# Two attention layers taken through five stages instead of four, with separate PSUM banks for maxima and scores and the rows normalised on GpSimd

## The reference

```
x: (32, 256, 256)   context: (32, 120, 256)   16 heads of width 16

layer 0:  h = layernorm(x)
          q = rope(h @ Wq); k = rope(context @ Wk); v = context @ Wv
          x = x + tanh(g[0]) * (softmax(q k^T / 4) v @ Wo + bo)

layer 1:  h = layernorm(layernorm(x)) * g + b;  c = layernorm(context) * g' + b'
          q = h @ Wq.T; k = c @ Wk.T; v = c @ Wv.T
          gate = sigmoid(h @ Wg.T + bg)
          x = x + tanh(g[1]) * ((softmax(q k^T / 4) v) * gate) @ Wo.T
```

## Time and profile before

| | |
|---|---|
| median of 3 runs | 3047.76 us (3045.49 to 3053.43) |
| the profiled execution | 3043.93 us, of which 3042.1 us are the span of the trace |
| busy over the whole span | PE 2019.0 us, DVE 1762.6, ACT 1315.4, POOL 1003.7 |
| attention, layer 0 | from the start to about 787 us |
| experts | to about 1515 us |
| attention, layer 1 | to about 2346 us |
| granted PE clock, mean over the execution | 0.81 |

### The profile page before, as it was taken

The page is one execution under the profiler, slowest core; times in us unless marked ns, Lnnn a source line. Parts: engine busy times, 40 slices in busy tenths (PEclk is TensorE's granted clock), DMA queues, the critical chain, the costliest instruction groups (busy, mean ns, idle before and its releaser), DMA issues. The chain is left out here.

```text
span 3042.1 us, 49795 instructions
## 1 busy us (share of the span) xinstructions
PE 2019.0 (66%) x14617; PEld 1560.7 (51%) x14617; DVE 1762.6 (58%) x3650; ACT 1315.4 (43%) x2345; POOL 1003.7 (33%) x1096
## 2 busy tenths in 40 slices
PE   5777677777543199999938788887886334444443
PEld 4555555555433199999825566665664222222222
DVE  5666666666454233333225555555553898988887
ACT  3444333344211044444324444444443566666665
POOL 0000100001266522222243333333330465565554
PEclk8988888888655599999968999999998566666666
DMA  2111111110443322222243333333331000000000
GB/s 68 40 36 43 36 39 36 37 43 26 141 154 125 123 76 87 87 87 87 77 82 65 69 80 71 69 68 67 76 70 56 17 27 28 28 21 28 28 25 17
DMA packets 177265, 185.56 MB, mean 61 GB/s; under 512 B 23745, under 2 KB 170946, under 8 KB 176130
## 3 DMA queue, kind: packets, MB, share of 16 engines
q1 hardware_dynamic: 152578, 149.49, 16.5%
q0 software_dynamic: 24576, 34.62, 5.6%
HBM read 109.82 MB, written 74.24 MB: 61 GB/s over the span
## 5 line engine op out<-in xcount | busy, mean ns | idle before, releaser
L527 DVE TENSOR_REDUCE a_mneg<-a_ps_s 128x8 f32<-128x960 f32 x256 | 285.8, 1151 | 63.0 <-PE a_ps_s L681 62.5
L681 PE MATMUL a_ps_s<-a_k,a_q 96*128 96x240 bf16 x1024 | 189.5, 334 | 153.9 <-DVE a_of L538 149.6
L377 ACT ACTIVATE a_probs<-a_ps_s 120x1024 f32<-120x1024 f32 x256 | 250.2, 1018 | 84.3 <-PE a_ps_s L695 84.3
L1295 DVE TENSOR_TENSOR e_h<-e_s,e_ps_ab 128x256 f32<-128x256 f32 (+1 forms) x213 | 89.4, 420 | 293.4 <-ACT e_s L1121 293.4
L1086 POOL TENSOR_TENSOR e_h_lo<-e_h 128x256 bf16<-128x256 f32 (+1 forms) x213 | 130.2, 611 | 326.0 <-DVE e_h L1295 326.0
L1314 PE MATMUL e_ps_ab<-e_xt_hi,e_w_hi 128*128 128x256 bf16 (+1 forms) x852 | 232.8, 273 | 0.1
L1314 PE MATMUL e_ps_ab<-e_xt_hi,e_w_lo 128*128 128x256 bf16 (+1 forms) x852 | 232.7, 273 | 0.0
L1314 PE MATMUL e_ps_ab<-e_xt_lo,e_w_hi 128*128 128x256 bf16 (+1 forms) x852 | 232.7, 273 | 0.0
L313 POOL TENSOR_TENSOR a_ve<-a_mv,a_eps 128x2 f32<-128x2 f32 x32 | 6.2, 195 | 664.7 <-DVE a_mv L506 664.7
L681 PEld LDWEIGHTS a_ps_s<-a_k,a_q 96*128 96x128 bf16 x1024 | 118.0, 121 | 195.2 <-DVE a_of L538 104.8
L341 POOL DMA_INDIRECT a_xa<-back_rows,a_where x128 | 202.2, 1580 | 45.8 <-issue 44.3
(11 more groups left out here) (237 smaller groups left out, 5430.8 us busy)
## 6 DMA issues: line engine op xcount, KB each, us to landing
e_xe<-sent_rows SPq DMA_DIRECT2D x71, 272.0 KB, 2.8
back_rows<-e_yo SPq DMA_DIRECT2D x71, 256.0 KB, 2.1
x_rows<-a_x SPq DMA_DIRECT2D x64, 256.0 KB, 3.2
a_xa<-in_x SPq DMA_DIRECT2D x32, 256.0 KB, 2.7
a_xr<-in_x SPq DMA_DIRECT2D x32, 256.0 KB, 2.9
e_xa<-x_rows SPq DMA_DIRECT2D x8, 1024.0 KB, 10.6
a_xa<-x_rows SPq DMA_DIRECT2D x32, 256.0 KB, 2.8
x_rows<-a_xa SPq DMA_DIRECT2D x32, 256.0 KB, 2.6
```

The source lines that it names most:

```text
L377: nc.scalar.activation(probs[0:S, 4 * g:4 * g + 4, :].rearrange("p h n -> p (h n)"), ps_s[0:S, g % 2, :, :].rearrange("p a n -> p (a n)"), ...
L527: nc.vector.tensor_reduce(mneg[:, g // 2, 8 * (g % 2):8 * (g % 2) + 8].rearrange("p (a h) -> p a h", a=2), ps_s[:, g % 2, :, 0:4 * S].rear ...
L681: last = nc.tensor.matmul(ps_s[:, g % 2, j // 2, (j % 2) * 2 * S:(j % 2 + 1) * 2 * S], q2[0:96, back.par, c, t * P:(t + 1) * P], k2[0:96, ...
```

## The change

There is one stage more, `mid`. It takes the maxima products, the maxima, their transposition and the gate projection out of `back` and `front`; `back` keeps the scores, the exponentials and the weighing. The order of the work in each engine's `step` is written anew.

- PSUM: `ps_m` (two banks, maxima) and `ps_e` (two banks, scores and weighed values) take the place of `ps_s`. The transposes of `raw` go to `ps_t` and `ps_x`.
- Maxima are taken for 4 heads at a time (eight instructions a batch in place of four), exponentials for two heads (eight of 512 columns for four of 1024), and the division is made in two halves.
- GpSimd computes `xn` and `cn`; the two gathers of layer 1 stand on both sides of it.
- The copy of query columns 4 to 7 (`q2b`) goes from DVE to ACT, and `xt` has two buffers.
- Signals `dv`, `da` and `de` belong to the stage `mid`; `tv` now covers the division too.

```diff
-        ps_s = psum("ps_s", [P, 2, 2, 512])
+        ps_m = psum("ps_m", [P, 2, 512])
+        ps_e = psum("ps_e", [P, 2, 512])
...
-                pipeline(eng, lambda *batches: step(None, *batches), 4, 6)
+                pipeline(eng, lambda *batches: step(None, *batches), 5, 6)
             else:
-                pipeline(eng, step, 5, 6)
+                pipeline(eng, step, 6, 8)
...
+                ng.wait(gp, pre, "rstd")
+                fe.wait(gp, pre.back(1), "xT")
+                nc.gpsimd.tensor_tensor(ready[:, :], half[:, 0:1], half[:, 0:1], ALU.mult).then_inc(ng.sem, 1)
+                for t in range(NT):
+                    last = nc.gpsimd.tensor_scalar(xn[:, t, :], xa[:, p, t, :], mv[:, t, 0:1], rstd[:, t:t + 1],
+                                                   ALU.subtract, ALU.mult)
+                if not first:
+                    last = nc.gpsimd.tensor_scalar(cn[0:S, :], ca[0:S, p, :], mv[0:S, NT, 0:1], rstd[0:S, NT:NT + 1],
+                                                   ALU.subtract, ALU.mult)
+                last.then_inc(ng.sem, 1)
...
+                def maxima():
+                    de.wait(act, mid, "mT")
+                    bv.wait(act, mid.back(1), "m_all")
+                    nc.scalar.activation(mt[:, :], ps_t[0:2 * H, 0:N // 2].bitcast(BF16), ACT.Copy).then_inc(da.sem, 1)
...
+                def turn_back(i):
+                    if i == 0:
+                        ba.wait(pe, tail, "raw")
+                        da.wait(pe, back, "mT")
                     else:
+                        fa.wait(pe, mid, "q2a")
+                        tv.wait(pe, tail.back(1), "sum")
+                    to = (ps_t, ps_x)[i]
+                    for g in range(H // GH):
+                        last = nc.tensor.transpose(to[:, g * P:(g + 1) * P], raw[:, g, i * P:(i + 1) * P], ident[:, :])
+                    last.then_inc(te.sem, 1)
...
+                def gate_rows():
+                    if t:
+                        tv.wait(pe, tail, "sum")
+                    elif f:
+                        fa.wait(pe, front.back(1), "q2a")
+                    for i in range(NT):
+                        last = product(ps_x[:, i * D:(i + 1) * D], terms(xt[:, mid.par, :, :], slice(i * P, (i + 1) * P), wq, D) + bias_terms)
+                    last.then_inc(de.sem, 1)
```

More of the change, by code:

```diff
@@ L186, in attention @@
         s_half = sem(tag + "half")
[L188 to L202, removed]
+        nv = Signal(sem(tag + "nv"), "stats mean")
@@ new lines, in attention @@
+        dv = Signal(sem(tag + "dv"), tops + " m_hi m_lo")
+        da = Signal(sem(tag + "da"), "mT" if first else "gate mT")
+        de = Signal(sem(tag + "de"), " ".join(f"ms{i}" for i in range(8)) + (" mT" if first else " g mT"))
+        bv = Signal(sem(tag + "bv"), "m_all")
+        ba = Signal(sem(tag + "ba"), " ".join(f"exp{i}" for i in range(NP)) + " raw")
+        be = Signal(sem(tag + "be"), " ".join(f"sc{i}" for i in range(NP)) + " pv")
+        tv = Signal(sem(tag + "tv"), "recip0 o0 recip1 o1 sum" if first else "recip0 o0 recip1 o1 gated sum")
@@ L310, in norms @@
             def norms(pre):
-                nv.wait(gp, pre, "mean1" if first else "mean2")
+                p = pre.par
+                nv.wait(gp, pre, "mean")
                 if first:
@@ L369, in _, with step, rows @@
             act.wait_ge(s_low, N_CONST_POOL)
[L371 to L386, removed]
+            def step(soon, pre, front, mid, back, tail):
+                f, m, b, t = front is not None, mid is not None, back is not None, tail is not None
+                def rows():
+                    p = front.par
+                    if first:
+                        fe.wait(act, front, "xT")
+                        fe.wait(act, front.back(2), "q")
+                        nc.scalar.activation(xt[:, p, :, :].rearrange("p k n -> p (k n)"), ps_q[:, :], ACT.Copy).then_inc(fa.sem, 1)
+                        return
                     fe.wait(act, front, "cT")
@@ L418, in keys @@
                                          ACT.Copy).then_inc(fa.sem, 1)
-                def maxima():
-                    be.wait(act, back, "mT")
-                    bv.wait(act, back.back(1), "m_all")
-                    nc.scalar.activation(mt[:, :], ps_t[0:2 * H, 0:N // 2].bitcast(BF16), ACT.Copy).then_inc(ba.sem, 1)
-                if f and not first:
-                    keys()
-                if b:
-                    maxima()
-                if f and first:
-                    keys()
                 def queries():
@@ L463, in step, with gating @@
                                          ACT.Copy, scale=pairmask[0:96, 0:1]).then_inc(fa.sem, 1)
+                    fe.wait(act, front, "qTb")
+                    nc.scalar.activation(q2[0:96, p, 4:8, :].rearrange("p c n -> p (c n)"), ps_kv[0:96, :].bitcast(BF16), ACT.Copy).then_inc(fa.sem, 1)
                     fe.wait(act, front, "qTa")
                     nc.scalar.activation(q2[0:96, p, 0:4, :].rearrange("p c n -> p (c n)"), ps_x[0:96, :].bitcast(BF16), ACT.Copy).then_inc(fa.sem, 1)
+                def gating():
+                    de.wait(act, mid, "g")
+                    tv.wait(act, mid.back(2), "gated")
+                    nc.scalar.activation(gate[:, mid.par, :, :].rearrange("p t d -> p (t d)"), ps_x[:, :], ACT.Tanh, scale=0.5).then_inc(da.sem, 1)
+                def maxima():
+                    de.wait(act, mid, "mT")
+                    bv.wait(act, mid.back(1), "m_all")
+                    nc.scalar.activation(mt[:, :], ps_t[0:2 * H, 0:N // 2].bitcast(BF16), ACT.Copy).then_inc(da.sem, 1)
+                if f:
+                    rows()
+                if b:
+                    for i in range(4):
+                        exp(i)
+                if t:
+                    result()
+                if b:
+                    exp(4)
+                if f:
+                    keys()
+                if b:
+                    exp(5)
+                    exp(6)
+                if f:
+                    queries()
+                if b:
+                    exp(7)
+                if m and not first:
+                    gating()
+                if f:
+                    values()
+                if b:
+                    turned_raw()
+                if f:
+                    columns()
+                if m:
+                    maxima()
             staged(nc.scalar, step)
```

532 lines of the change are left out of this document (274 added, 258 removed).

## The result

The changed kernel takes 3131.41 us (median of 4 runs, 3126.0 to 3133.52), the kernel before, beside it on the same chip, 3049.76 (4 runs). The ratio is 1.0266, with a 95% interval of 1.0245 to 1.0286. The forecast was 3132. That nearness is luck: the change to layer 0 gained some 44 us more than forecast, the one to layer 1 cost some 44 more, and the two errors cancel.

What follows compares the result with a forecast made beforehand. No engine but a ring of waits bounds the kernel. Steps of 21.0 and 28.8 us against 23.80 and 23.94, 29 each, plus 12 a layer, give -69 and +153; with 3043.9 and 3.8 that makes 3132, range 2980 to 3200.

Steps and rivals of the forecast that it cites:

- The clock ahead of the gate: Layer 1, gate projection after PE waits for the sum: low clock adds 1.2 us a step, between 1.0 and 1.8.
- Item (4) of the ring of layer 1: Layer 1, ACT after the gate projection: gate 0.6, then the values, for which the weighing waits; 1.05 us.
- item (3) of layer 0: Layer 0, ACT ahead of the weighing: query copy, last exponential and values, 1.5 us.
- both rings: Chains of last-ending waits through one step, at full clock: 19.1 us in layer 0, 25.75 us in layer 1.
- The clock at the step's end: Both layers, PE pausing during ACT's final copies: the clock drop costs 1.9 us a step.
- The partial steps: Each layer: the thirtieth full step becomes two partial ones of 18.0 us, 12 us more a layer.
- -69 and +153: Forecast changes in us for the whole of layer 0 and of layer 1, together +84.
- Clock stays high: Both layers: no clock drops because the idle stretches are partly broken up; -60 us, 2988 in all; chance 0.12.
- Clock lost twice over: Both layers: larger clock losses, steps of 21.8 and 30.2 us; +148 us, 3195 in all; chance 0.15.
- A shorter ring in layer 1: Layer 1: drops fall where something else is waited for, step 26.0 us; +3 us, 3050 in all; chance 0.12.
- The stages decouple: Both layers: PE alone sets the steps, 17.2 and 19.6 us; -292 us, 2756 in all; chance 0.08.
- GpSimd blocks DVE: Layer 0 key rotation: GpSimd's normalisations hold up DVE's two-input sum; 35 us more, 3167 in all; chance 0.03.

Runs made afterwards that it cites:

- the filled run: Changed kernel with 28 unread identity transposes on PE before its wait for the sum in layer 1: 3024.54 us, ratio 0.9923.
- the version with all three moves: Changed kernel with the layer 1 sum early, ACT's key columns copied early and the upper query copy back on DVE: 2755.53 us, ratio 0.9043.

## Why the prediction was right, and where it was not

**The mechanism held.** The new order puts the sum behind the seventh and eighth groups of maxima and the query split, and PE waits for it: forecast about 3.2 us, measured 3.01 in the step above and 3.1 in the mean. Removing that position alone gives 217 us back. The step's end also hangs on ACT's chain of copies, as forecast: with the key copy out of it, the step is 1.8 and 2.3 us shorter. But a second chain, DVE's key columns and the transposed maxima, ends only 0.5 us ahead of ACT's copies, which the forecast did not see.

**The clock ahead of the gate was mis-sized.** The term was 1.2 us, bounded 1.0 to 1.8. It measures 4.5 in the step shown and 10.25 - 5.85 = 4.4 in the mean, and the filled run gives back 3.8 in all: outside the bounds. I had taken the gate projection alone as slow, and that by a row misread. Of the two rows of eight matmuls in the earlier trace rows I called the one of 2.77 us "at the low clock". The stretch around it (columns as above) says otherwise:

```profile
19.00:22.30 3.30, 3.22 (x9) 1.95 (x7) 1.28 (x5) 0.80 (x2) 0.00 (x0) 1.00 0.38 107
```

The granted clock is 1.00 there. So 2.77 against 1.89 is no ratio of the two levels; what made that row longer is not known. At the low level four matmuls of the gate projection take 2.08 us, and 1.13 at the high one, so the projection lost not 0.9 but 2.9 us. And the low level held almost 10 us, through the key transposes and most of the weighing. Over 29 steps that is 29 x (4.5 - 1.2) = 96 us, more than the 44 by which layer 1 is dearer than forecast; the next three points take the rest back.

**The weighing does not wait for the values of this step.** Item (4) of the ring of layer 1, and item (3) of layer 0, let ACT's values end before the weighing. In the trace of after, ACT's values (line 443) wait for the weighing's end instead, 104.8 us in 28 steps, because the copy frees its buffer there. They delay PE's query transposes by 0.51 us, and raw by 0.28. So both rings were counted too long. Taking the clock terms out of the measured steps gives 19.90 - 1.35 = 18.55 in layer 0 against my 19.1, and 30.63 - 4.5 - 1.55 = 24.6 in layer 1 against 25.75.

**The clock at the step's end** is 1.35 and 1.55, where I took 1.9 for both. Together with the shorter ring this makes layer 0 the 1.1 us a step better that was measured.

**The partial steps** were a term of +12 a layer and measure about 0 and 3. A partial step of before was the wrong row. The last two raw copies of a layer are 10.4 to 10.6 us apart in the changed kernel (657.3 to 667.7, and 2413.6 to 2424.2), against 18.0.

Summed up, the forecast was -69 and +153; the runs give -113 and +197. Their sums, both +84 (81.65 measured side by side), agree because the errors cancel. The direction and the wait were foreseen; the number was luck.

**GpSimd.** The pair of normalisations was put between 0.4 and 1.2 us and takes 2.45, so the upper bound was wrong:

```profile
L331 POOL TENSOR_SCALAR a_xn<-a_xa,a_mv,a_rstd 128x256 f32<-128x256 f32 x128 | 156.9, 1230 | 0.0
```

One takes 1.23 us, twice the subtraction of the earlier trace rows. In the running steps it has no waiter all the same (PE waits for it only at a layer's start), and the cover of some 12 us that the forecast named holds it easily.

**The rivals.** "Clock stays high" falls: the mean clock of layer 1 is 0.78. "Clock lost twice over" comes near in layer 1 (30.2 a step, measured 30.63), but by wrong terms, 2.7 at the step's end and 1.8 ahead of the gate where 1.55 and 4.5 were measured, and not in layer 0 (21.8, measured 19.90). "A shorter ring in layer 1" falls with 30.63: the ring was shorter, but the drops were not covered. "The stages decouple" is no case of this kernel, but its time of 2756 is what the version with all three moves reaches. That is a coincidence: its steps are 17.12 and 20.52 where the rival had 17.2 and 19.6, and PE does not set them. It is idle for 17.12 x (1 - 400.57/480) = 2.8 us of a step in layer 0 and 20.52 x (1 - 353.88/400) = 2.4 in layer 1, above the 2 us together that I gave as the condition. "GpSimd blocks DVE" falls: DVE's key rotation reads two tensors in SBUF while GpSimd normalises (414.27 to 416.72), and its sum takes 0.42 us, as in the kernel before (second row below). The first row is of the changed kernel. Over all 32 steps its median is 0.43, the longest 0.69.

```profile
415.21 0.42 DVE L589 TENSOR_TENSOR a_kf<-a_k_cos,a_k_sin 120x256 f32<-120x256 f32 x1
```

```profile
391.38 0.42 DVE L583 TENSOR_TENSOR a_kf<-a_k_cos,a_k_sin 120x256 f32<-120x256 f32 x1
```

The Trainium skill ("SBUF — State Buffer", SBUF: two separate sides) would have it blocked until the GpSimd instruction ends; the first row does not agree. Its rule did agree with the earlier trace rows, where another kind of instruction ran on both engines: DVE's normalisation, begun at 401.98 while this sum of GpSimd ran in the kernel before:

```profile
401.82 1.26 POOL L326 TENSOR_TENSOR a_xb<-a_xr,a_bias 128x512 f32<-128x512 f32 x1
```

## What to carry to other kernels

When stages are pipelined on engines that work in order, place each instruction that frees a buffer right behind the one that makes its input: here 0.74 us of work standing 3 us too late cost 217 us of 3131. Count what lies between the step's last result and the instruction that the next step starts with, on every chain that ends there: taking a copy out gave its whole 0.94 us once, and only 0.52 where another chain came next. A copy whose input is ready earlier should go ahead. Price a pause of PE by the work that runs after it at the low clock, read through to where the clock is back, and not by the pause alone.

## What the hardware showed

- After one pause of 3.0 us the granted clock was at 0.50 for almost 10 us of unbroken work, which took 4.5 us longer for it, more than the pause itself. Before, in the same layer, a pause of 2.73 us cost about 1.2, as the prediction works out, and a drop at a step's start of the changed layer 0 costs 1.6. So the length of the pause alone does not give the price.
- Transposes that nobody reads, put into a pause, pay here: 107 us in layer 1 ahead of the gate, 83 us at the steps' ends, 28.9 us even in a kernel that was already at 0.97 of full clock in both layers.
- GpSimd's normalisation (one input tensor and two scalars from memory) takes 1.23 us for 256 columns; its subtraction of two tensors takes 0.61, and DVE does two normalisations in 0.73.
- Halving the tiles of the maxima cost DVE little: two of 480 columns take 1.22 us, two of 960 took 2.22, so a batch pays 4 x 1.22 - 2 x 2.22 = 0.44 us more.
